# Row tiles 10 and 11 transposed on TensorE, the last four by DMAs on SyncE's queue, with a new order of the first stage

## What is computed

```python
def fake_quant(x, scale, zp):
    q = jnp.clip(jnp.round(x / scale + zp), 0.0, 255.0)
    return (q - zp) * scale
x = x + tanh(g_xattn) * matmul(fake_quant(layernorm(x)), fake_quant(ctx))
h = layernorm(x)
base = einsum('bsd,od->bso', h, base_W)
probs = softmax(einsum('bsd,ed->bse', h, router_W))
w_dense = weights of the top 2 of 8 experts, normalised
mid = einsum('bsd,edr->bser', h, lora_A) * w_dense[..., None]
x = x + tanh(g_ffn) * (base + 2.0 * einsum('bser,erd->bsd', mid, lora_B))
```

## Time and profile before

| | us |
|---|---|
| three runs | 1079.86, 1085.41, 1085.31 (median 1085.31) |
| the profiled execution, its own time | 1081.69 |
| its span | 1080.0 |
| TensorE busy | 1029.1 |
| mean granted clock over the span | 0.993 of full |

### The profile page before, as it was taken

The page is one execution under the profiler, slowest core; times in us unless marked ns, Lnnn a source line. Parts: engine busy times, 40 slices in busy tenths (PEclk is TensorE's granted clock), DMA queues, the critical chain, the costliest instruction groups (busy, mean ns, idle before and its releaser), DMA issues.

```text
span 1080.0 us, 13035 instructions
## 1 busy us (share of the span) xinstructions
PE 1029.1 (95%) x5008; PEld 769.6 (71%) x5008; DVE 786.5 (73%) x1102; ACT 467.5 (43%) x492; POOL 208.7 (19%) x123
## 2 busy tenths in 40 slices
PE   1899999899899999999999999999999999999998
PEld 1344444344598787888887888898788888888887
DVE  7897797769368765567678677977877797755554
ACT  7883654420142232223544445554444555443432
POOL 2245553299604333400000000000000000000000
PEclk9999999999999999999999999999999999999999
DMA  9884898978668867673585885868578585668765
GB/s 367 311 320 161 330 313 297 236 246 300 228 231 324 308 242 263 247 252 107 174 314 182 276 279 175 277 192 312 182 265 290 165 284 188 204 194 308 240 198 180
DMA packets 97678, 269.04 MB, mean 249 GB/s; under 512 B 19792, under 2 KB 27984, under 8 KB 89936
## 3 DMA queue, kind: packets, MB, share of 16 engines
q1 hardware_dynamic: 67472, 231.50, 61.9%
q10 hardware_dynamic: 30144, 36.71, 11.1%
HBM read 214.70 MB, written 50.33 MB: 245 GB/s over the span
## 4 chain that ended last, share of the span: by engine, by line
PE 68%; DVE 16%; DMA 6%; issue 4%; POOL 3%; ACT 2%; ACTq 0%; SPq 0%; DVEq 0%; POOLq 0%
PE acc L1383 16%; PE acc L1385 16%; PE acc L1384 15%; PE acc L1361 10%; DVE w_lo L1105 4%; DMA w_stage<-in_wt 3%; PE aT_psum L1453 2%; DVE bn_chunks_group L972 2%; PE aT_psum L1432 1%; PE aT_psum L1431 1%; DVE S_sum L1201 1%; DVE S_lo L1209 1%; DVE c_acc L1179 1%; POOL t_job L687 1%; DMA x_scratch<-x_group_odd 1%
## 5 line engine op out<-in xcount | busy, mean ns | idle before, releaser
L1105 DVE TENSOR_TENSOR w_lo<-w_stage,w_hi 128x1024 fp32r<-128x1024 f32 x200 | 248.8, 1256 | 160.0 <-ACT w_hi L807 159.0
L807 ACT ACTIVATE w_hi<-w_stage 128x1024 fp32r<-128x1024 f32 x200 | 209.2, 1058 | 341.9 <-PE acc L1385 289.4
L1383 PE MATMUL acc<-w_hi,S_hi 128*128 128x512 f32 x384 | 151.4, 394 | 3.1 <-DVE w_lo L1105 2.7
L1385 PE MATMUL acc<-w_hi,S_lo 128*128 128x512 f32 x384 | 149.7, 390 | 0.0
L1384 PE MATMUL acc<-w_lo,S_hi 128*128 128x512 f32 x384 | 149.5, 389 | 0.0
L1361 PE MATMUL acc<-ctx_quant,aT_even 128*128 128x512 bf16 x512 | 117.1, 390 | 7.5 <-DVE ctx_quant L1019 7.4
L1361 PE MATMUL acc<-ctx_quant,aT_odd 128*128 128x512 bf16 x512 | 114.0, 384 | 5.1 <-issue 5.1
L1383 PE MATMUL acc<-w_hi,A_hi 128*128 128x512 f32 x288 | 114.0, 396 | 0.3
L1385 PE MATMUL acc<-w_hi,A_lo 128*128 128x512 f32 x288 | 112.4, 390 | 0.0
L1384 PE MATMUL acc<-w_lo,A_hi 128*128 128x512 f32 x288 | 112.2, 390 | 0.0
L687 POOL TENSOR_TENSOR t_job<-t_job 128x1024 f32<-128x1024 f32 x32 | 85.9, 2685 | 125.9 <-DMA t_job<-in_wt 124.7
(11 more groups left out here) (179 smaller groups left out, 1590.5 us busy)
## 6 DMA issues: line engine op xcount, KB each, us to landing
w_stage<-in_wt SPq DMA_DIRECT2D x104, 512.0 KB, 4.5
w_stage<-w_sums_scratch SPq DMA_DIRECT2D x96, 512.0 KB, 4.3
ctx_stage<-in_ctx SPq DMA_DIRECT2D x32, 1024.0 KB, 7.4
t_job<-in_wt SPq DMA_DIRECT2D x8, 2048.0 KB, 11.4
w_sums_scratch<-t_job SPq DMA_DIRECT2D x8, 2048.0 KB, 11.7
c_acc<-x_scratch SPq DMA_DIRECT2D x32, 512.0 KB, 5.7
out<-c_acc ACTq DMA_DIRECT2D x64, 256.0 KB, 5.0
...
```

The lines of the kernel that those rows point to most:

```text
L807: ins = act.activation(wh[i % HI][:, :], raw[:, :], ACT.Copy)
L1105: ins = dve.tensor_tensor(low[:, :], raw[:, :], high[:, :].bitcast(F32), ALU.subtract)
L1383: pe.matmul(out_, lh, rh, start=first, stop=False, skip_group_check=onto)
L1385: return pe.matmul(out_, ll, rh, start=False, stop=final, skip_group_check=onto)
```

## The change

Tables of slots, LOAD_ORDER, UNIT_TILE and UNIT_BLOCK are all new (64 units as before; tiles 12 to 15 still from unit 44 on; blocks 4 and 5 ahead of 6 and 7). PE_TILES goes from 10 to 12 and WIDEN_ACT from 7 to 11 tiles. The transposing DMAs of tiles 12 to 15 go from ScalarE to SP, behind the last load. The column sums get one more addition on VectorE and half the matmuls. The ring of raw weight buffers is turned by two, job 1 and job 2 get other room, and SP loads pieces 0 to 3 before it waits for jobs 1 and 2. The last x1 store and the row work of group 1 in the second stage get other places. The slot tables are cut here to a few; of the others, the first evacuation goes from slot 40 to 37, and the four conversions of block 1 stay at 48 to 57 (49 to 55 after).

```diff
@@ -61,49 +61,49 @@
-LOAD_ORDER = 'xxccxccccxcccxcccccxcccxcxxcxcccxcxccccccxxcccxx'
+LOAD_ORDER = 'xxccxcccxccccccxccccxcccxxxxcccxccxccxcccxcxccxc'
...
-UNIT_TILE = [0, 1, 2, 0, 1, 2, 3, 0, 1, 2, 0, 1, 2, 3, 3, 3, 4, 5, 6, 7, 4, 5, 6, 7, 4, 5, 6, 7, 4, 5, 6, 7, 8,
-    9, 10, 8, 9, 10, 11, 11, 8, 9, 10, 11, 12, 13, 12, 8, 9, 10, 11, 14, 15, 13, 14, 15, 12, 13, 14, 15, 12, 13,
-    14, 15]
+UNIT_TILE = [0, 1, 2, 0, 1, 2, 3, 3, 0, 1, 2, 3, 4, 0, 1, 2, 3, 5, 4, 5, 6, 7, 6, 7, 4, 5, 6, 7, 4, 5, 6, 7, 8,
+    9, 8, 9, 10, 10, 11, 11, 8, 9, 10, 11, 12, 12, 13, 13, 8, 9, 10, 11, 14, 15, 14, 15, 12, 13, 14, 15, 12, 13,
+    14, 15]
...
-UNIT_BLOCK = [0, 0, 0, 1, 1, 1, 1, 2, 2, 2, 3, 3, 3, 3, 2, 0, 0, 0, 0, 0, 1, 1, 1, 1, 3, 3, 3, 3, 2, 2, 2, 2, 5,
-    5, 5, 6, 6, 6, 6, 5, 4, 4, 4, 4, 4, 4, 5, 7, 7, 7, 7, 4, 4, 5, 5, 5, 7, 7, 7, 7, 6, 6, 6, 6]
+UNIT_BLOCK = [0, 0, 0, 1, 1, 1, 0, 1, 2, 2, 2, 2, 0, 3, 3, 3, 3, 0, 1, 1, 0, 0, 1, 1, 2, 2, 2, 2, 3, 3, 3, 3, 4,
+    4, 5, 5, 4, 5, 4, 5, 6, 6, 6, 6, 4, 5, 4, 5, 7, 7, 7, 7, 4, 4, 5, 5, 6, 6, 6, 6, 7, 7, 7, 7]
...
-WIDEN_ACT = [2, 3, 4, 8, 9, 13, 15]
+WIDEN_ACT = [1, 2, 3, 4, 5, 8, 11, 12, 13, 14, 15]
...
-PE_TILES = 10
+PE_TILES = 12
...
-STATS_SLOT = [0, 2, 15, 34, 63, 95, 123, 131, 178, 191, 222, 236, 302, 309, 327, 334]
+STATS_SLOT = [0, 2, 12, 39, 67, 103, 135, 149, 180, 183, 225, 244, 290, 308, 332, 344]
...
-STD_SLOT = [1, 5, 19, 41, 70, 105, 125, 133, 182, 200, 230, 240, 304, 313, 336, 341]
+STD_SLOT = [1, 5, 29, 42, 77, 112, 140, 151, 182, 185, 230, 250, 294, 316, 337, 348]
...
-WIDEN_SLOT = [10, 18, 33, 62, 88, 141, 148, 158, 194, 216, 249, 256, 315, 331, 355, 367]
+WIDEN_SLOT = [9, 13, 40, 65, 96, 125, 160, 164, 205, 238, 258, 262, 304, 340, 352, 364]
...
-CU_SLOT = [3, 9, 16, 20, 28, 36, 47, 53, 56, 65, 74, 80, 91, 97, 107, 110, 179, 185, 188, 201, 219, 224, 234,
-    237, 271, 276, 279, 286, 291, 308, 317, 318]
+CU_SLOT = [3, 8, 17, 22, 27, 32, 44, 52, 56, 59, 69, 79, 84, 88, 97, 105, 189, 191, 196, 209, 214, 219, 228,
+    237, 241, 291, 297, 309, 310, 321, 331, 343]
...
-MOVE_SLOT = [13, 21, 37, 66, 98, 152, 164, 171, 209, 225, 253, 260, 323, 337, 361, 372]
+MOVE_SLOT = [11, 26, 43, 70, 99, 129, 166, 176, 216, 245, 270, 279]
...
-COPY_SLOT = [17, 23, 44, 71, 101, 159, 166, 173, 214, 231]
+COPY_SLOT = [24, 30, 47, 72, 107, 130, 170, 178, 224, 247, 272, 280]
...
-STORE_SLOT = [161, 119, 155, 150, 204, 245, 284, 250, 358, 344, 343, 399, 413, 430, 455, 443]
+STORE_SLOT = [102, 114, 136, 161, 233, 234, 246, 267, 317, 328, 356, 398, 412, 421, 439, 452]
...
-JOB_SLOT = [338, 359, 375, 386, 394, 400, 405, 414, 418, 424, 432, 438]
+JOB_SLOT = [388, 393, 399, 404, 415, 422, 427, 433, 440, 445, 449, 453]
...
@@ -124,7 +124,7 @@
...
 JOBS_A = 3
-FILL_AT = (8, 9, 10, 11, 12, 13, 16, 17)
+FILL_AT = (8, 9, 10, 11, 13, 14, 16, 17)
 JOB_LOAD = {0: 3, 4: 4, 9: 5, 13: 6, 18: 7}
...
@@ -305,15 +305,16 @@
...
         arv = [at(f"ar_hi_lo{r}", CST + 4 * KIB * r, [P, WK, 2, AR], F32R) for r in range(HI)]
-        wst = [at(f"w_stage{r}", CST + 24 * KIB + 4 * KIB * r, [P, WK * NW], F32) for r in range(RAW)]
-        wl = [at(f"w_lo{r}", CST + 24 * KIB + 4 * KIB * r, [P, WK * NW], F32R) for r in range(RAW)]
+        raw_at = [CST + (24 + 4 * ((r + 2) % RAW)) * KIB for r in range(RAW)]
+        wst = [at(f"w_stage{r}", raw_at[r], [P, WK * NW], F32) for r in range(RAW)]
+        wl = [at(f"w_lo{r}", raw_at[r], [P, WK * NW], F32R) for r in range(RAW)]
         mids = at("mid_scaled", SMALL + 20 * KIB, [P, M, E, R], F32)
...
 
-        job_at = [CST, SMALL + 4 * KIB, CST + 16 * KIB, XG0 + 16 * KIB, XG0, XG0 + 16 * KIB, XG0,
+        job_at = [CST, CST + 16 * KIB, AT0, XG0 + 16 * KIB, XG0, XG0 + 16 * KIB, XG0,
                   XG0 + 16 * KIB]
...
@@ -395,6 +396,7 @@
...
         block_ready = sem("block_ready")
+        sums_ready = sem("sums_ready")
         col_ready = sem("col_ready")
...
@@ -447,6 +449,12 @@
...
 
+        def wait_transposed(eng, t):
+            if t < PE_TILES:
+                eng.wait_ge(tp_ready, t + 1)
+            else:
+                eng.wait_ge(aT_moved[t % 2], 16 * sum(w % 2 == t % 2 for w in range(PE_TILES, t + 1)))
+
         def wait_aT(eng, t):
...
@@ -544,17 +552,21 @@
...
 
+            def aT_move(t):
+                g, m = t // M, t % M
+                if g >= 2:
+                    sp.wait_ge(pe_unit, last_of_tile(t - 2 * M) + 1)
+                wait_widened(sp, t)
+                sp.dma_start_transpose(aT[g % 2][:, :, m * P:(m + 1) * P], anat[t % 2][:, :])\
+                    .then_inc(aT_moved[t % 2], 16)
+
             def load_job(j):
...
                 if j == 1:
-                    if PE_TILES:
-                        sp.wait_ge(tp_ready, PE_TILES)
-                    for t in range(max(PE_TILES, TILES - 2), TILES):
-                        wait_aT(sp, t)
-                    sp.wait_ge(col_ready, 2 * NB)
+                    wait_transposed(sp, TILES - 2)
                 if j == 2:
-                    sp.wait_ge(c_conv, 2 * NB * CP)
+                    sp.wait_ge(pe_unit, max(last_of_tile(t) for t in range(2 * M, 3 * M)) + 1)
                 if j in (3, 4):
...
@@ -600,31 +612,37 @@
...
                     load_ctx(LOAD_ORDER[:i].count("c"))
+            for t in range(PE_TILES, TILES):
+                aT_move(t)
             load_job(0)
             load_job(1)
+            store_job(0)
+            wait_transposed(sp, TILES - 1)
+            sp.wait_ge(col_ready, 2 * NB)
+            for i in range(4):
+                load_piece(i)
             load_job(2)
-            store_job(0)
             store_job(1)
+            sp.wait_ge(job_stored[1], 16)
+            load_piece(4)
+            load_piece(5)
             store_job(2)
-            sp.wait_ge(job_stored[1], 16)
-            sp.wait_ge(job_stored[2], 16)
-            for i in range(RAW - 1):
-                load_piece(i)
-            for a in range(2):
-                sp.wait_ge(x1_stored[a], 16 * NB * 2)
-            load_res(0, 1, 0)
-            load_res(0, 1, 1)
             for i, (g, kind, s, pc) in enumerate(PIECES):
-                if i + RAW - 1 < N_PIECES:
+                if 1 <= i < N_PIECES - RAW + 1:
                     load_piece(i + RAW - 1)
+                if i == 4:
+                    for a in range(2):
+                        sp.wait_ge(x1_stored[a], 16 * NB * 2)
+                    load_res(0, 1, 0)
+                    load_res(0, 1, 1)
                 if g == 0 and kind == "W":
...
                         store_job(JOB_STORE[at_piece])
-                    if at_piece in (1, 2, 3, 7):
-                        load_row(1, (1, 2, 3, 7).index(at_piece))
+                    if at_piece in (1, 2, 3, 5):
+                        load_row(1, (1, 2, 3, 5).index(at_piece))
                     if s > 1 and pc == 1:
...
@@ -754,14 +772,6 @@
...
 
-            def aT_move(t):
-                g, m = t // M, t % M
-                if g >= 2:
-                    act.wait_ge(pe_unit, last_of_tile(t - 2 * M) + 1)
-                wait_widened(act, t)
-                act.dma_start_transpose(aT[g % 2][:, :, m * P:(m + 1) * P], anat[t % 2][:, :])\
-                    .then_inc(aT_moved[t % 2], 16)
-
             def store_x1(i):
...
@@ -778,8 +788,6 @@
...
                     aT_copy(COPY_AT[s])
-                if s in MOVE_AT and MOVE_AT[s] >= PE_TILES:
-                    aT_move(MOVE_AT[s])
                 if s in QUANT_AT:
...
@@ -815,14 +823,16 @@
...
                 h_hi(k)
-                if k == 1:
-                    store_x1(LAST_STORE)
                 if k % WK == WK - 1:
                     w_hi(HI - 1 + k // WK)
+                if k == 5:
+                    store_x1(LAST_STORE)
 
...
                 act.wait_ge(fill_done, done + 1)
+                if done == 0:
+                    act.wait_ge(job_stored[2], 16)
                 if done == 16 * (g - 1):
...
@@ -884,8 +894,8 @@
...
                         act.activation(mth[:, :], colp[:, :], ACT.Copy).then_inc(mth_ready, 1)
-                    if at_piece in (6, 8, 10, 14):
-                        row_std(1, (6, 8, 10, 14).index(at_piece))
+                    if at_piece in (5, 6, 11, 13):
+                        row_std(1, (5, 6, 11, 13).index(at_piece))
                     if at_piece - 1 in FILL_AT:
...
@@ -1026,6 +1036,9 @@
...
                     .then_inc(block_ready, 1)
+                dve.wait_ge(block_ready, c + 1)
+                dve.tensor_tensor(pair[:, 0:K // 4, :], pair[:, 0:K // 4, :], pair[:, K // 4:K // 2, :], ALU.add)\
+                    .then_inc(sums_ready, 1)
 
...
@@ -1235,14 +1248,12 @@
...
                         router(chain, 0, 2 * at_piece + 1)
-                    if at_piece == 5:
-                        row_stats(chain, 1, 0)
                     if at_piece == 6:
                         mid_lo(0)
-                    if at_piece in (7, 9, 11, 15):
-                        row_normalise(chain, 1, (7, 9, 11, 15).index(at_piece))
```

(37 more changed lines are left out.)

30 lines of the change are left out of this document (5 added, 25 removed).

## The result

The changed kernel takes **1077.02 us** (median of 9 runs, 1073.06 to 1080.72) against 1085.31 before (9 runs, 1079.86 to 1089.28): ratio 0.9929, 95% interval 0.9903 to 0.9955. It is faster by 0.7%, where 1064 (2%) was forecast; the range held it. The profiled execution took 1076.38, span 1074.6.

The account below looks back on a forecast made before the run. TensorE's work plus some 51 us of standing was taken as the bound. Terms -6.9 + 1.8 - 5.0 + 0 - 1.8 - 4.0 + 1.0 - 4.5 gave -19.4 us, forecast 1064 us, range 1054 to 1078.

Parts of the forecast that it names:

- The hand-over: Between unit 63 and the first AR product: weight pieces loaded early leave 2.8 us of VectorE work, 2.3 us gained.
- the clock: Behind the change to the second stage: TensorE idles only 1.5 us, so its clock stays up, 1.7 us gained.
- Piece 6: In the AR product: this weight load waits for POOL's 12th job step, fits by 7 us; 1.0 us added.
- Tile 12: Before unit 44: the transposed x tile comes earlier, a wait of about 2 us remains, 5.0 us gained.
- rival A: Transposes stay slow: tile 12 lands 19.4 us after issue, TensorE waits 12.5 us, 1076 us in all; chance 0.13.
- Rival B: VectorE or ScalarE holds TensorE, giving back half the column-sum saving and 3 us at the start: about 1071; chance 0.20.
- The start: Up to the end of unit 5: reordered conversions and copies cost 0, ends -3 and +3 us.
- The two tiles more on TensorE: Tiles 10 and 11 transposed on TensorE at 0.89 us each, 1.8 us added, their ScalarE copies hidden.
- the -6.9: Column sums on TensorE: 4 matmuls instead of 8, eight times, 6.9 us less, VectorE staying about even.
- The second stage: Row normalisations moved to other pieces remove two waits for c_acc: 4.5 us gained, ends -5.1 and 0.
- Rival C: SP's four transposes in one chain need 13 to 19 us each, delaying tile 15 and job 0: 1091 us; chance 0.05.

Follow-up runs that it names:

- Run 8: Changed kernel with POOL starting its last but one job step only after VectorE's three first AR splits: 1080.39 us, 0.9956 of the kernel before.
- run 6: Changed kernel with tiles 12 to 15 transposed on TensorE too, all sixteen there: 1075.37 us, 0.9926 of the kernel before.
- run 7: Changed kernel with the four transposing DMAs issued by ScalarE instead of SP: 1076.84 us, 0.9942 of the kernel before.
- run 9: As run 8, with the store of job 2 also moved behind the AR pieces in SP's queue: 1072.14 us, 0.9894 of the kernel before.
- run 2: Changed kernel with POOL's last two job steps and the store of job 2 moved behind the AR product: 1072.57 us, 0.9886 of the kernel before.
- run 3: Changed kernel with VectorE's three first splits moved ahead of the evacuations of units 62 and 63: 1078.33 us, 0.9941 of the kernel before.
- run 4: Changed kernel without the second addition of the pair sums, column sums of 8 matmuls again: 1078.34 us, 0.9957 of the kernel before.
- run 5: Kernel before with only the halved column sums added (second VectorE addition, 4 matmuls): 1082.54 us, 0.9968 of the kernel before.
- run 10: Changed kernel with the second stage's work on the rows of group 1 and the fills put back as before: 1085.49 us, 1.0008 of the kernel before.

## Why the prediction was right in sign and wrong in size

**The hand-over (-4.0, of it -2.3 for the hand-over itself and -1.7 for the clock) is the step that failed: the hand-over came to +2.9 and the AR product behind it to +1.1.** The prediction priced it as "evacuation 63 (0.75), three splits (0.83 for two), the split of the first transposed column block (0.69)" from rows in which POOL stood still, and in the changed kernel POOL's last two job steps and a column add lie exactly there. The prediction had POOL's end five us behind the last unit (measured 6.3) and charged it to piece 6 alone, not to VectorE. Run 8 shows the price without POOL beside it: 2.5 us. In the kernel before, POOL's last step ended at 279.1, eight us ahead of the last unit's end, and its last column add before the first split (289.72):

```profile
276.80 2.35 POOL L687 TENSOR_TENSOR t_job<-t_job 128x1024 f32<-128x1024 f32 x1
...
288.44 1.26 POOL L678 TENSOR_TENSOR x_group_odd<-x_group_odd,col_term 128x512 f32<-128x512 f32 x1 [2.19 <-DVE x_group_odd L1042]
```

The new slots moved the steps, and run 6 shows that SP's transposes have no part in that. The Trainium skill (SBUF — State Buffer, SBUF: two separate sides) says that VectorE and GpSimd share one port pair as an exclusive lock, held for a whole instruction, and that a VectorE operation with two SBUF inputs is subject to it against a GpSimd operation that reads SBUF. The trace agrees as to which operations stand (splits yes, hT_lo no) and, in most profiles, as to how long: one POOL operation for each split. In two profiles (the changed kernel's and run 7's) one split stood through three. The price could have been had from the rows: two job steps and a column add are 2.55 + 1.47 + 2.55 = 6.6 us, with the evacuation, the last split and hT_lo (0.75 + 0.4 + 0.69) 8.4 us; 8.0 was measured.

**The clock went with it.** "TensorE then idles only 1.5 us ... so the 1.7 of clock come too" was right as a mechanism: behind 6.7 us it was at 0.50 for the next 5.4 us, behind 1.2 us (runs 8, 9) and 2.3 us (run 2) it stayed at 1.00. The AR product lost 1.1 us instead of gaining 1.7.

**Piece 6 (+1.0) was the right place and the wrong size.** It was said to fit by 7 us; with the short hand-over TensorE stood 6.24 and 6.45 us for it (runs 3, 8). In run 8, counted from the last unit's end (285.20), the piece lands at 19.8 us where 13 was said: POOL's last step ends 8.1 us behind instead of 5, and the piece takes 11.3 us to land instead of 8. TensorE runs out of work at 15.1 us where 19.8 was said, since the piece's split stands in ScalarE's and VectorE's queues well ahead of its use, in front of what TensorE needs next. And from the landing to the matmul are 1.8 us more. 6.8 + 4.7 + 1.8 is the 13.3 us between the two: 6.8 were said to be in hand, and TensorE stood 6.45. In the changed kernel the long hand-over hid this wait: there SP issues piece 6 only at 294.10, when its buffer comes free, 6.1 us after it had issued the store. These are two limits in series. Taking away the first alone is worth nothing (0.9956), both 0.9894. The second was not taken away alone; since SP waits for the buffer in the changed kernel, nothing should come of it there. With both away the forecast for these two stages holds to 0.4 us.

**Tile 12 (-5.0).** The wait of 2 us was forecast and is 1.81, at full clock behind it (1.00), but by luck: the tile and TensorE both came late. Counted from the end of unit 31, the tile is there at 50.1 us, where 44 to 46 were said, and TensorE comes to it at 48.3, where 44.9 were said. Of these 3.4 us, 2.8 are the waits for the pair sums at 174.38 and 197.13; they cost nothing more, as TensorE would have stood for tile 12 instead. The transposing DMA of tile 12 was issued at 191.4 and landed 18.9 us later, which is rival A's landing (19.4) without a job load beside it. Most of it is the queue: SP's last load, c31, issued just ahead at 190.93, landed at 202.6, and the tile 7.7 us behind it, the 6 to 8 that were said. What was mis-sized is the end of the loads, 42.4 us after the end of unit 31 and not 38. The core moved 341 to 343 GB/s from 190 to 200 us, where 421 was taken, and part of that was a 1 MB store of group 2, issued at 192.04. Rival A's wait of 12.5 us did not come, since it counted the whole landing from 38 us and not from the issue at 31.

**Rival B (VectorE holds TensorE) came true in part.** The second pass takes 1.22 us where it is alone (forecast 1.4), 2.17 and 2.88 where POOL runs beside it, so TensorE waits 1.83 and 0.99. POOL's column add ends at 173.24 and its row term at 195.99, each 1.1 us before the end of the pass beside it. TensorE's saving of 0.87 per sum was exact, but of 6.9 us only some 2 reached the hand-over by the profile of run 4, and in the kernel before none can be told (run 5).

**The start (0) cost 1.0**, within its ends. The copy of the first transposed tiles is waited for until 27.30, as forecast (unit 0 begins at 28.96, 28.7 was said), but the copy of the third now stands behind ScalarE's conversions (wait of 4.09). Both come in place of two waits for ctx_quant. Unit 5 ends at 62.3, where 61.5 was said and 61.3 was measured before.

**The two tiles more on TensorE (+1.8) were right**: their transposes start at 163.69 and 168.04, and the next units 0.90 and 0.89 us later.

**The sum counts two column sums twice.** The start at 0 was worked out with the two sums before the end of unit 5 already halved, and the -6.9 takes the same two off again, 1.7 us too much. The other way, the stretches of the kernel before are 0.8 us longer than the prediction's prices make them. That is the 0.9 between 1061.5 and 1060.6. With the two sums counted once the sum would be -17.7 us and not -19.4.

**The second stage (-4.5) was right**: 5.1 us by the profiles before and after, 5.1 and 6.0 by run 10 against the two profiles of the changed kernel, and it is most of the change's gain. The waits for c_acc went as the prediction named them (5.1 to 0.6); a wait for x_rows of 1.3 is new.

**Rival C (one chain of SP) did not come**: the four went out between 191.4 and 222.8 us, and no unit waited for tiles 13 to 15. That they were moved to SP is worth nothing measurable (run 7).
